# Attention and expert kernel on one core: the scan's filter stored in natural order, the context reversed instead, two heads' filter tiles loaded directly, a paired router, a fifth bank for blocks, and new orders on all engines

## The chip, the cores and the metric

The kernel runs on one core of a Trainium2 chip. The engines are TensorE (PE), VectorE (DVE), ScalarE (ACT), GpSimd (POOL) and SyncE (SP), which issues most DMAs. The metric is the device time of one execution in microseconds.

## What is computed

The reference takes x and a context (8 sequences of 128 channels by 256 steps), normalises x, and combines them in 16 heads of 8 channels: for every pair of channels of a head the product of two context rows is convolved causally with the head's filter, the filter's tap D is added, and the result is multiplied with the query and summed. The result is added to x, normalised again, and goes through a mixture of 8 experts with the best two chosen per row.

```python
kv = einsum('bhil,bhjl->bijhl', k, v)              # k = v = context, by head
y = irfft(rfft(kv, 2L) * rfft(ssm_kernel, 2L))[..., :L]
out = einsum('bijhl,bhil->bjhl', y + kv * D, q)    # q = layernorm(x)
x = x + tanh(g_xattn) * out
z = layernorm(x)
gates = top-2 of softmax(z @ router_w + router_b), normalised
combined = sum over e of gates[e] * gelu(z @ expert_w[e] + expert_b[e])
x = x + tanh(g_ffn) * (combined @ out_w + out_b)
```

## The kernel before, in words

The order of every engine is written out by hand, and the engines meet in semaphores. The program has these stages.

*Start.* Filter taps and D are loaded, VectorE reverses the taps and adds D to the first one, and SP writes them, with 128 zeros behind, to a scratch in DRAM (`kpad_dram`). Five DMAs (`TOEP`) read it back with overlapping rows, which gives the Toeplitz tile `toep` of each head. Context and x come in four loads each (`context_in`, `x_in`), two of each on ScalarE's queue and two on SP's. TensorE transposes the context as it comes (`context(i)`), ScalarE evacuates it to `ctxT`. VectorE takes the statistics of the first four sequences of x, GpSimd the power -1/2 of their variances (`first_inverse_std`), VectorE writes the scaled queries in reversed order (`backwards`), and TensorE transposes them (`queries(i)`). `WARM_UP` says how many transposes without a use TensorE does between these.

*Convolutions.* There are 32 items n: two groups of four sequences (g = n // 16) by 16 heads. `products` multiplies pairs of context channels (on GpSimd, for the items in `BY_VECTOR` on VectorE) into one of six slots, `convolve(n)` is two fp32 products with `toep` into one of four banks (`ring`), and `query_products(n)` on VectorE (four instructions) multiplies with the queries into `zq` and frees the bank (`read_out`).

*Sums.* `sum_channels(b)` adds the slots of `zq` by transposes that accumulate, for one sequence. `fold` adds one half of the slots to the other beforehand, so that fewer transposes are left: one fold in the first group (8 slots become 7), four in the second, two by VectorE and two by GpSimd (`FOLDED_BY_DVE`, `FOLDED_BY_POOL`). `residual(b)` on VectorE adds x from memory and frees the bank of the sum. ScalarE takes statistics, normalises, TensorE transposes z, and high and low parts of z are taken (`z_high`, `z_low`).

*Experts.* A block (b, k) is one sequence by two experts, six matmuls of 512 columns in `experts(n, b, k)`. There are 32, the first 16 for the sequences 0 to 3. ScalarE does the gelu in the bank, VectorE multiplies with the gates and adds (`accumulate`), which frees the bank. The experts' weights are made relative to their last row (`relative`), then split into a high part (ScalarE, `split_weights`) and a low part (`weights_low`). The router has six matmuls (`route_logits`), its logits are transposed back (`route_rows`), and VectorE picks the two best and makes the gates (`choose_values`, `choose_experts`, `weigh`). At last the mixture is transposed, split and projected (`mix_transposed`, `mix_low`, `project`, `finish`).

The sums of the second group stand on TensorE behind the first four blocks, and wait for all folds:

```python
for n in range(4, 7):
    sum_channels(n)        # behind experts(3)
experts(4, *BLOCKS[4])
sum_channels(7)
```

## Time and profile before

| | us |
|---|---|
| median of 3 runs (lowest, highest) | 116.19 (115.92, 118.51) |
| the profiled execution | 115.83 |
| its span, first to last instruction | 114.0 |
| TensorE busy in it | 103.2 |
| VectorE busy | 90.2 |
| GpSimd busy | 63.0 |
| ScalarE busy | 57.2 |

The span is what the views of the trace cover; the 1.8 us between it and the execution's own time lie around it. All times of a row are counted from the span's start. TensorE's busy time counts matmuls that overlap one another, so the distance between the starts of two rows says more about its pace than the length of one. An engine's idle time costs something only where TensorE, or whoever it waits for, is late because of it.

### The profile page before, as it was taken

Reading aid. Unit: us, or ns where it says so; the run is one execution under the profiler, and the core shown is the slowest. Engines: PE = TensorE matmul, PEld = TensorE weight load, DVE = VectorE, ACT = ScalarE, POOL = GpSimd, SP = SyncE. Lnnn points to the kernel's source line nnn. Section 1 sums busy time; section 2 is a strip of 40 time slices with the busy share of each in tenths; the row PEclk is TensorE's granted clock in tenths of the full one; section 3 lists DMA queues with packets and bytes.
Section 4 is the critical chain, followed back from the end, with each engine's and each line's share of the span. In section 5 each row is a group of like instructions: output and inputs, shape, how many; then the busy total and the mean of one; then the engine's idle time right before and its main releaser. Section 6 shows DMA issues by size and latency. Waiting matters only on the chain.

```text
span 114.0 us, 1919 instructions
## 1 busy us (share of the span) xinstructions
PE 103.2 (90%) x574; PEld 86.3 (76%) x574; DVE 90.2 (79%) x293; ACT 57.2 (50%) x145; POOL 63.0 (55%) x83
## 2 busy tenths in 40 slices
PE   4956999989999999996679999999999999999960
PEld 4945888868999887754568888886788888888940
DVE  0283899999999998999889969777588876866940
ACT  4074377064258718641469997465645424353300
POOL 3015799999999999999999899600000000000000
PEclk9999999999999999999999999999999999999997
DMA  2867999159872410030030000000000101111031
GB/s 79 294 165 196 297 370 324 50 180 244 227 231 87 155 35 3 0 92 0 0 95 6 0 0 0 0 0 0 0 6 0 46 11 35 46 49 46 0 98 46
DMA packets 10956, 10.02 MB, mean 88 GB/s; under 512 B 1306, under 2 KB 10946, under 8 KB 10946
## 3 DMA queue, kind: packets, MB, share of 16 engines
q1 hardware_dynamic: 9570, 8.85, 26.6%
q10 hardware_dynamic: 1376, 1.05, 2.9%
q8 instruction: 5, 0.08, 0.3%
q14 instruction: 5, 0.04, 0.1%
HBM read 8.82 MB, written 1.07 MB: 87 GB/s over the span
## 4 chain that ended last, share of the span: by engine, by line
PE 61%; POOL 17%; DVE 13%; ACT 4%; issue 3%; POOLq 0%; DVEq 0%
PE ring L835 11%; PE ring L837 11%; PE ring L836 11%; POOL kv_t L374 10%; PE ring L756 6%; DVE zq_t L397 4%; PE ring L757 3%; PE ring L706 3%; DVE ow_lo_t L1040 2%; POOL w_lo_t L389 2%; ACT q_t L560 2%; PE red L779 2%; POOL rstd L403 2%; PE zbank L877 2%; PE red L712 2%
## 5 line engine op out<-in xcount | busy, mean ns | idle before, releaser
L1116 DVE SCALAR_TENSOR_TENSOR mix_t<-ring,ctxT_t,mix_t 128x256 f32<-128x256 f32 x55 | 26.6, 484 | 7.8 <-ACT ring L603 6.1
L603 ACT ACTIVATE ring<-ring 128x512 f32<-128x512 f32 (+1 forms) x33 | 18.7, 568 | 20.7 <-PE ring L837 20.7
L374 POOL TENSOR_TENSOR kv_t<-ctxT_t 128x320 f32<-128x320 f32 x27 | 23.7, 908 | 8.2 <-ACT ctxT_t L515 6.5
L835 PE MATMUL ring<-w_hi_t,zT_hi_t 128*128 128x512 f32 (+1 forms) x66 | 26.1, 396 | 0.0
L837 PE MATMUL ring<-w_hi_t,zT_lo_t 128*128 128x512 f32 (+1 forms) x66 | 25.4, 385 | 0.0
L836 PE MATMUL ring<-w_lo_t,zT_hi_t 128*128 128x512 f32 (+1 forms) x66 | 25.4, 384 | 0.0
L756 PE MATMUL ring<-kv_t,toep_t 128*128 128x288 f32 x64 | 20.9, 409 | 0.2 <-DVE zq_t L1021 0.2
L757 PEld LDWEIGHTS ring<-kv_t,toep_t 128*128 128x128 f32 x64 | 12.2, 190 | 3.3
L837 PEld LDWEIGHTS ring<-w_hi_t,zT_lo_t 128*128 128x128 f32 x66 | 12.4, 188 | 2.5
L835 PEld LDWEIGHTS ring<-w_hi_t,zT_hi_t 128*128 128x128 f32 x66 | 12.5, 189 | 2.3
L836 PEld LDWEIGHTS ring<-w_lo_t,zT_hi_t 128*128 128x128 f32 x66 | 12.5, 189 | 2.1
L779 PE MATMUL red<-ident,zq_t 128*128 128x128 f32 x88 | 11.3, 280 | 2.7 <-POOL zq_t L397 1.5
L1016 DVE TENSOR_TENSOR zq_t<-ring,qT_t 128x256 f32<-128x256 f32 x32 | 13.3, 415 | 0.1
L779 PEld LDWEIGHTS red<-ident,zq_t 128*128 128x128 f32 x88 | 10.5, 194 | 3.7 <-issue 2.7
L757 PE MATMUL ring<-kv_t,toep_t 128*128 128x144 f32 x64 | 13.1, 286 | 0.0
L1018 DVE TENSOR_TENSOR zq_t<-ring,qT_t 128x192 f32<-128x192 f32 x32 | 11.1, 347 | 0.0
L756 PEld LDWEIGHTS ring<-kv_t,toep_t 128*128 128x128 f32 x64 | 9.9, 191 | 0.4 <-issue 0.4
L389 POOL TENSOR_TENSOR w_lo_t<-ctx_t,w_hi_t 128x512 fp32r<-128x512 f32 x7 | 9.4, 1355 | 0.0
L549 ACT ACTIVATE w_hi_t<-ctx_t 128x512 fp32r<-128x512 f32 x8 | 5.0, 621 | 3.9 <-POOL ctx_t L383 3.9
L706 PE MATMUL ring<-ident 128*128 128x128 f32 x25 | 5.4, 372 | 1.6 <-POOL ident L453 1.6
L397 POOL TENSOR_TENSOR zq_t<-zq_t 128x1024 f32<-128x1024 f32 x2 | 6.7, 3371 | 0.0
L397 DVE TENSOR_TENSOR zq_t<-zq_t 128x1024 f32<-128x1024 f32 x3 | 5.9, 2006 | 0.0
(124 smaller groups left out, 170.8 us busy)
## 6 DMA issues: line engine op xcount, KB each, us to landing
ctx_t<-in_L_ffn_expert_w SPq DMA_DIRECT2D x8, 256.0 KB, 4.3
toep_t<-kpad_dram SPq DMA_DIRECT2D x3, 512.0 KB, 6.6
x_t<-in_x SPq DMA_DIRECT2D x8, 128.0 KB
out<-x_t SPq DMA_DIRECT2D x8, 128.0 KB
wlast_t<-in_L_ffn_expert_w SPq DMA_DIRECT2D x1, 768.0 KB, 7.1
ctx_t<-in_ctx ACTq DMA_DIRECT2D x2, 256.0 KB, 3.0
zq_t<-in_x ACTq DMA_DIRECT2D x2, 256.0 KB, 3.7
ctx_t<-in_ctx SPq DMA_DIRECT2D x2, 256.0 KB, 4.2
```

Source lines behind the costliest of these rows:

```text
L374: eng.tensor_tensor(dst, head.unsqueeze(1).to_broadcast([P, HB + 1, HD * CB]), windows(ctxT_t, g, h, HB + 1), ALU.mult).then_inc(done, 1)
L389: eng.tensor_tensor(w_lo[:, :, e, :], raw[:, e % RAW], w_hi[:, :, e, :].bitcast(F32), ALU.subtract).then_inc(done, 1)
L397: eng.tensor_tensor(terms[:, i], terms[:, i], terms[:, HB + i], ALU.add).then_inc(done, 1)
L603: act.activation(y, y, ACT.Gelu_apprx_tanh).then_inc(gelu_ready, 1)
L756: pe.matmul(y, within, src, start=True, stop=False)
L757: pe.matmul(y[:, :, BG:CB], past, src[:, :, 0:BG], start=False, stop=True).then_inc(convolved, 1)
L779: last = pe.matmul(red[b % 2][:, P * c:P * (c + 1)], zq[:, g, i, :, BG * c + b % BG], ident[:, :], is_transpose=True, start=(i == 0), stop ...
L835: pe.matmul(y, hi, whi, start=(c == 0), stop=False)
L836: pe.matmul(y, hi, wlo, start=False, stop=False)
L837: last = pe.matmul(y, lo, whi, start=False, stop=(c == C - 1))
L1016: dve.tensor_tensor(terms(HB * P, [[P * CB, HB]], H, HD), pairs, windows(qT_t, g, h, HB).rearrange("p d (i a) -> p d i a", i=HD), ALU.mult)
L1116: dve.scalar_tensor_tensor(out=acc, in0=ring[n % RING][:, L * e:L * (e + 1)], scalar=gate, in1=acc, op0=ALU.mult, op1=ALU.add).then_inc(mi ...
```

## The change

The filter is stored in natural order, without VectorE's reversal: the taps are loaded behind 127 zeros, GpSimd adds D, and the halves of the Toeplitz tile change places. What must now be reversed is the context: ScalarE writes each load reversed in time (`turn(i)`), and TensorE transposes that copy. Queries and residuals are no longer reversed. x is first on ScalarE's queue, and the first two context loads go to SP's. The item order within a group begins with head 1 (`FIRST`), and the tiles of heads 1 and 2 (`DIRECT`) don't go through the scratch: one DMA behind the scratch write reads them from the taps in DRAM, GpSimd masks what lies outside, and VectorE adds D (`add_direct`). The first group is no longer folded. The router's high and low parts stand side by side (`rw_pair`), so that four matmuls do what six did; the two halves of the result are added in `route_rows` by products with a doubled identity (`twice`). Block 4 writes to `obank` instead of a ring bank, and the later blocks move up by one bank. VectorE takes over the relative step of experts 1 and 3 and the low part of expert 1 and gives back the low part of expert 5. The orders on all engines are new; TensorE does five blocks before the first two sums of the second group, and VectorE has the low part of the projection behind block 5.

The core of the diff:

```diff
-TOEP = ((0, 1), (1, 3), (4, 4), (8, 4), (12, 4))
-BY_VECTOR = (0, 5, 15, 22, 27)
-
-RELATIVE_BY_DVE, LOW_BY_DVE = (), (5,)
-FOLDED_BY_DVE = ((2,), (2, 3))
+FIRST, DIRECT = 1, 2
+TOEP = ((3, 2), (5, 3), (8, 4), (12, 4), (0, 1))
+BY_VECTOR = (2, 3, 9, 14, 23)
+
+RELATIVE_BY_DVE, LOW_BY_DVE = (1, 3), (1,)
+FOLDED_BY_DVE = ((), (2, 3))
 FOLDED_BY_POOL = ((), (0, 1))
-WARM_UP = (12, 1, 6, 1, 5, 5)
+FOLDS = ((4, 0), (5, 1), (6, 2), (7, 3), (2, 0), (3, 1), (1, 0))
+WARM_UP = (14, 1, 26, 1, 1, 5)
...
+        def item(n):
+
+            return n // H, (n + FIRST) % H
+
+        def block_bank(n):
+
+            return obank if n == RING else ring[(n - (n > RING)) % RING]
...
             sp.wait_ge(scratch_written, 16)
             for i, (h, n) in enumerate(TOEP):
-                src = bass.AP(scratch.tensor, h * (P + L), [[1, P], [P + L, n], [1, L]])
+                src = bass.AP(scratch.tensor, h * (P + L - 1), [[1, P], [P + L - 1, n], [1, L]])
                 sp.dma_start(toep[:, h:h + n, :], src).then_inc(toeplitz_in[i], 16)
-                if i >= len(TOEP) - 3 and i < len(TOEP) - 1:
-                    load(sp, xn, x, x_in, i - len(TOEP) + 5)
...
+            for i in range(2):
+                load(sp, cv, ctx_in, context_in, i)
+            sp.wait_ge(taps_ready, 1)
             sp.wait_ge(constants_ready, 1)
             sp.dma_start(scratch, kpad[:, :]).then_inc(scratch_written, 16)
+            src = bass.AP(ssm_kernel.tensor, FIRST * L - (P - 1), [[1, P], [L, DIRECT], [1, L]])
+            sp.dma_start(toep[:, FIRST:FIRST + DIRECT, :], src).then_inc(direct_in, 16)
             for i in range(2, LOADS):
                 load(sp, cv, ctx_in, context_in, i)
+            for i in range(2, LOADS):
+                load(sp, xn, x, x_in, i)
...
+                pool.wait_ge(direct_in, 16)
+                within = toep[:, FIRST:FIRST + DIRECT, 0:P]
+                pool.affine_select(out=within, in_=within, compare_op=ALU.is_ge, fill=0.0, base=1 - P,
+                                   pattern=[[0, DIRECT], [1, P]], channel_multiplier=1).then_inc(direct_masked, 1)
                 pool.wait_ge(first_queries_ready, BG)
...
-            for i in range(2):
-                load(act, cv, ctx_in, context_in, i)
-            for i in range(2):
-                load(act, xn, x, x_in, i)
+            load(act, xn, x, x_in, 0)
+            load(act, xn, x, x_in, 1)
+            act.dma_start(direct_d, everywhere(ssm_d, FIRST, DIRECT)).then_inc(direct_d_in, 16)
...
+            def turn(i):
+
+                act.wait_ge(context_in[i], 16)
+                start = CB * HD * P + B * L + BL * i * L
+                act.activation(backwards(zq_t, G * CB * HD * P, start),
+                               cv[:, BL * i:BL * (i + 1), :].rearrange("p b (c n) -> p b c n", c=C),
+                               ACT.Copy).then_inc(context_turned, 1)
...
+            def block_bank_free(n):
+
+                if n < RING:
+                    pe.wait_ge(read_out, 2 * H - RING + n + 1)
+                elif n == RING:
+                    pe.wait_ge(z_low_ready, BG - 1)
+                else:
+                    pe.wait_ge(mixed_in, 2 * (n - RING + (n > 2 * RING)))
...
+                both = [rw_pair[:, 2 * E * c:2 * E * (c + 1)] for c in range(C)]
+                pe.matmul(red[0][0:2 * E, :], both[0], zT_hi[:, own, 0, :], start=True, stop=False)
                 for c in range(C):
-                    for n, (w, z) in enumerate(((rw_hi, zT_hi), (rw_hi, zT_lo), (rw_lo, zT_hi))):
-                        last = pe.matmul(red[0][0:E, :], w[:, E * c:E * (c + 1)], z[:, own, c, :],
-                                         start=(c == 0 and n == 0), stop=(c == C - 1 and n == 2))
-                last.then_inc(logits_ready, 1)
+                    pe.matmul(red[0][0:E, :], both[c][:, 0:E], zT_lo[:, own, c, :], start=False, stop=False)
+                pe.matmul(red[0][0:2 * E, :], both[1], zT_hi[:, own, 1, :], start=False,
+                          stop=True).then_inc(logits_ready, 1)
...
-                    last = pe.transpose(red[1][:, E * b:E * (b + 1)], lgT_sb[:, P * b:P * (b + 1)], ident[0:E, 0:E])
+                    last = pe.matmul(red[1][:, E * b:E * (b + 1)], lgT_sb[:, P * b:P * (b + 1)], twice[:, :],
+                                     start=True, stop=True)
...
-            for i in range(LOADS):
+            for i in range(2):
                 context(i)
                 warm_up(WARM_UP[i + 1], ring[RING - 1])
             queries(0)
             queries(1)
-            for n in range(0, 16):
+            context(2)
+            context(3)
...
+            def add_direct():
+
+                dve.wait_ge(direct_masked, 1)
+                dve.wait_ge(added_d_ready, 1)
+                within = toep[:, FIRST:FIRST + DIRECT, 0:P]
+                dve.tensor_tensor(within, within, added_d, ALU.add).then_inc(direct_ready, 1)
```

Two places of the order matter for what follows. The first is TensorE's start. Before, with `red` the banks of the context's transposes, `ring` that of the warm-ups, `zbank` and `obank` those of the queries:

```order
L706 MATMUL ring<-ident 128x128 x12
L712 MATMUL red<-ident,ctx_t 128x128 x4
L706 MATMUL ring<-ident 128x128
L712 MATMUL red<-ident,ctx_t 128x128 x4
L706 MATMUL ring<-ident 128x128 x6
L712 MATMUL red<-ident,ctx_t 128x128 x4
L706 MATMUL ring<-ident 128x128
L712 MATMUL red<-ident,ctx_t 128x128 x4
L706 MATMUL ring<-ident 128x128 x5
L712 MATMUL zbank<-ident,q_t 128x128 x2
```

And now, where `zq_t` holds the turned context:

```order
L762 MATMUL ring<-ident 128x128 x14
L768 MATMUL red<-ident,zq_t 128x128 x4
L762 MATMUL ring<-ident 128x128
L768 MATMUL red<-ident,zq_t 128x128 x4
L762 MATMUL ring<-ident 128x128 x26
L768 MATMUL zbank<-ident,q_t 128x128 x2
L768 MATMUL obank<-ident,q_t 128x128 x2
L768 MATMUL zbank<-ident,q_t 128x128 x2
L768 MATMUL obank<-ident,q_t 128x128 x2
L768 MATMUL red<-ident,zq_t 128x128 x8
L820 MATMUL ring<-kv_t,toep_t 128x288
```

The second half of the context has moved behind the queries, to just before the first convolution, and 26 warm-ups stand where there were six and one and five.

The second place is VectorE behind the last query product of the second group. Before, with the folds on top, the low part of the projection (`ow_lo_t`), and then the choice of experts:

```order
L397 TENSOR_TENSOR zq_t<-zq_t 128x1024 x2
L1040 TENSOR_TENSOR ow_lo_t<-ow_t,ow_hi_t 128x512
L1060 MAX zbank<-red 128x8 x4
...
L1029 TENSOR_TENSOR x_t<-red,x_t 128x256
L1113 TENSOR_SCALAR mix_t<-ring,ctxT_t 128x256
L1116 SCALAR_TENSOR_TENSOR mix_t<-ring,ctxT_t,mix_t 128x256
L1029 TENSOR_TENSOR x_t<-red,x_t 128x256
```

And now:

```order
L428 TENSOR_TENSOR zq_t<-zq_t 128x1024 x2
L1136 MAX zbank<-red 128x8 x4
...
L1189 TENSOR_SCALAR mix_t<-ring,ctxT_t 128x256
L1192 SCALAR_TENSOR_TENSOR mix_t<-ring,ctxT_t,mix_t 128x256
L1189 TENSOR_SCALAR mix_t<-ring,ctxT_t 128x256
L1192 SCALAR_TENSOR_TENSOR mix_t<-ring,ctxT_t,mix_t 128x256
L1105 TENSOR_TENSOR x_t<-red,x_t 128x256 x2
```

The low part of the projection has left this place for one behind block 5, and two blocks are mixed in ahead of the first two residuals. On TensorE the sums of the second group, which were three in one piece (24 transposes) behind block 3 and one behind block 4, now are two behind block 4 and two behind block 5.

## Rows read from the trace of the kernel before

**Rows 1.** Head of the page: busy time, share of the span, instructions of each engine.

```profile
PE 103.2 (90%) x574; PEld 86.3 (76%) x574; DVE 90.2 (79%) x293; ACT 57.2 (50%) x145; POOL 63.0 (55%) x83
```

**Rows 2.** Busy time by stretch: us, engines, granted clock, DMA share, GB/s.

```profile
4.30:7.40 3.10, 3.05 (x16) 2.81 (x14) 1.90 (x7) 0.98 (x3) 0.00 (x0) 1.00 0.54 130
12.40:28.90 16.50, 16.09 (x92) 13.60 (x91) 16.09 (x69) 8.40 (x26) 16.14 (x22) 1.00 0.80 236
28.90:45.50 16.60, 16.53 (x115) 14.65 (x113) 15.92 (x67) 9.46 (x29) 16.36 (x24) 1.00 0.41 125
53.00:59.10 6.10, 3.37 (x26) 2.89 (x25) 5.43 (x24) 2.29 (x8) 6.03 (x7) 1.00 0.15 44
61.40:77.40 16.00, 16.00 (x76) 13.19 (x76) 13.34 (x31) 12.09 (x28) 11.31 (x15) 1.00 0.00 0
```

**Rows 3.** Timeline of the start: start us, duration us, engine, line, operation.

```profile
1.64 2.82 PE L706 MATMUL ring<-ident 128*128 128x128 f32 x12 [1.64 <-POOL ident L453]
5.40 0.43 DVE L966 BATCH_NORM_STATS2 zq_t<-zq_t 128x6 f32<-128x256 f32 x1 [1.26 <-DMA zq_t<-in_x]
6.18 0.64 PE L706 MATMUL ring<-ident 128*128 128x128 f32 x2
6.97 0.38 PE L706 MATMUL ring<-ident 128*128 128x128 f32 x2
9.24 1.02 POOL L403 TENSOR_TENSOR rstd<-vareps,neghalf 128x4 f32<-128x4 f32 x1
12.49 0.65 PE L756 MATMUL ring<-kv_t,toep_t 128*128 128x288 f32 x2
```

**Rows 4.** Timeline of 47 to 65 us: VectorE, GpSimd and TensorE.

```profile
47.53 4.71 DVE L397 TENSOR_TENSOR zq_t<-zq_t 128x1024 f32<-128x1024 f32 x2
47.76 6.71 POOL L397 TENSOR_TENSOR zq_t<-zq_t 128x1024 f32<-128x1024 f32 x2
52.17 2.85 DVE L1040 TENSOR_TENSOR ow_lo_t<-ow_t,ow_hi_t 128x512 fp32r<-128x512 f32 x1
54.62 1.13 PE L779 MATMUL red<-ident,zq_t 128*128 128x128 f32 x8 [1.46 <-POOL zq_t L397]
54.94 0.39 DVE L1060 MAX8 zbank<-red 128x8 f32<-128x8 f32 x4
57.68 0.41 DVE L1029 TENSOR_TENSOR x_t<-red,x_t 128x256 f32<-128x256 f32 x1
62.84 0.39 PE L835 MATMUL ring<-w_hi_t,zT_hi_t 128*128 128x512 f32 x1
64.21 0.39 PE L835 MATMUL ring<-w_hi_t,zT_hi_t 128*128 128x512 f32 x1
```

**Rows 5.** DMA issues with KB and median us to landing; one evacuation of ScalarE.

```profile
ctx_t<-in_ctx ACTq DMA_DIRECT2D x2, 256.0 KB, 3.0
zq_t<-in_x ACTq DMA_DIRECT2D x2, 256.0 KB, 3.7
gains<-in_g_xattn ACTq DMA_DIRECT2D x1, 0.5 KB, 3.9
6.42 0.60 ACT L513 ACTIVATE ctxT_t<-red 128x512 f32<-128x512 f32 x1 [4.42 <-PE red L712]
```

**Rows 6.** Timeline of 28 to 40 us; last row: a form of the groups.

```profile
28.89 5.13 PE L779 MATMUL red<-ident,zq_t 128*128 128x128 f32 x42
30.30 0.79 DVE L1051 CAST rw_hi<-rw_t 128x16 fp32r<-128x16 f32 x1 [0.23 <-POOL rw_t L435]
36.87 0.65 PE L756 MATMUL ring<-kv_t,toep_t 128*128 128x288 f32 x2
38.60 0.41 DVE L1016 TENSOR_TENSOR zq_t<-ring,qT_t 128x256 f32<-128x256 f32 x1
39.40 0.41 DVE L1016 TENSOR_TENSOR zq_t<-ring,qT_t 128x256 f32<-128x256 f32 x1
L389 DVE TENSOR_TENSOR w_lo_t<-ctx_t,w_hi_t 128x512 fp32r<-128x512 f32 x1 | 0.8, 760 | 0.0
```

More of the change, by code:

```diff
@@ L467, in _ @@
+            products(pool, 15, pool_products_ready)
+            products(pool, 16, pool_products_ready)
+            relative(pool, 0, weights_relative)
+            for n in range(17, 20):
                 products(pool, n, pool_products_ready)
+            weights_low(pool, 0, weights_low_ready)
+            products(pool, 20, pool_products_ready)
+            relative(pool, 2, weights_relative)
             ones()
-            router_relative_rows()
-            products(pool, 23, pool_products_ready)
@@ L482, in _ @@
-            relative(pool, 2, weights_relative)
-            relative(pool, 3, weights_relative)
-            weights_low(pool, 2, weights_low_ready)
+            products(pool, 21, pool_products_ready)
+            products(pool, 22, pool_products_ready)
+            products(pool, 24, pool_products_ready)
+            weights_low(pool, 2, weights_low_ready)
+            for n in range(25, 29):
+                products(pool, n, pool_products_ready)
+            router_relative_rows()
+            scales(2)
@@ L647, in _ @@
             activate(3)
+            activate(4)
+            split_weights(6)
+            projection_high()
             statistics(B + 4)
-            split_weights(4)
-            statistics(B + 5)
-            statistics(B + 6)
-            activate(4)
-            split_weights(5)
-            statistics(B + 7)
             activate(5)
-            split_weights(6)
+            for n in range(5, 8):
+                statistics(B + n)
             activate(6)
@@ L775, in sum_channels @@
                     pe.wait_ge(pool_folded, sum(len(i) for i in FOLDED_BY_POOL[:g + 1]))
[L776 removed]
+                gone = [FOLDS[i][0] for i in FOLDED_BY_DVE[g] + FOLDED_BY_POOL[g]]
+                slots = [i for i in range(HD) if i not in gone]
                 for c in range(C):
```

364 lines of the change are left out of this document (194 added, 170 removed).

## The prediction

> **What bounds the kernel now.** The first view to read is the head of the page [rows 1]: TensorE is busy 103.2 us (90% of the span), VectorE 90.2. That alone says little, so the second is the busy time by stretch [rows 2]. It cuts the run at the places where the character changes. From 12.4 us to 45.5 TensorE has work almost without a break (16.09 of 16.50, 16.53 of 16.60). From 53.0 to 59.1 it has 3.37 of 6.10, and after 61.4 it is full again (16.00 of 16.00). VectorE is as full up to 59 us (16.09, 15.92, 5.43), and only after that it has slack (13.34 of 16.00). So there are three places where time can come from: the start, up to the first convolution; TensorE's hole of 53 to 59 us; and work taken off TensorE. An edit on another engine pays only through one of these.
>
> The third view is the timeline of the start [rows 3]. VectorE begins the statistics of x at 5.40, when x lands. GpSimd takes a product first and comes to its power of the variance only at 9.24 (1.02 us); the scale, four query rows and their transposes follow, and the first convolution runs at 12.49. Call that moment T.
>
> The fourth is the timeline around the hole [rows 4]. VectorE ends its last query product at 47.5 and starts two folds (4.71 us), while GpSimd does two (6.71 us). GpSimd's second ends at 54.5, and TensorE, which has run out of blocks, starts the channel sums of the second group at 54.62. The third sum waits again, because its bank is read by the residual of 57.68, which stands on VectorE behind the low part of the projection (52.17, 2.85 us) and the gates (from 54.94). The seventh expert block (n = 6) starts at 62.84.
>
> **The start.** x is first on its queue: issued at 0.74 instead of 1.78. The context took 3.0 us from that place, x 3.7 us from the later one [rows 5], so x is there at about 3.7. Four rows of statistics (0.43 and a short aggregation each, some 0.52) and the variance end at 6.0 [rows 3]. GpSimd has no product ahead of its power now, but it has the masking of D, which waits for a small load: issued at about 1.8 with the 3.9 us of the gains [rows 5] that is 5.7, and with 0.3 to 0.6 us for the mask 6.2. So the power runs 6.3 to 7.3. The scale also needs the tanh on ScalarE, and that stands behind the turned context: two loads issued at 1.6 and 2.1 on SP land like x did (5.3 and 5.9); two turns of 128x512. The trace has no turn; the nearest row is ScalarE's copy of 128x512 out of a bank, 0.60 us [rows 5], and the bounds are half of it, if reading elsewhere is cheaper, and twice, if the reversed order halves the rate. I take 0.55. Transposes to 7.0; half the evacuation is that copy and one of half its size, to 7.85; tanh and scale are tiny, 8.35; the query rows are ready at 9.1 and 9.75. TensorE does 26 warm-up transposes after the context's: at 0.11 us (two in 0.38, of which the last lasts 0.27 [rows 3]) that is 7.1 to 9.96. Then 16 transposes (queries 0 and 1, context 2 and 3), 1.75 us: T = 11.7, 0.8 earlier. The first GpSimd product is there by 10.7. The direct Toeplitz load is issued at 4.5, lands with the 3.0 to 3.7 us of the other loads by 8.2, and its mask (to 8.8) and the adding of D on VectorE (half of the 0.76 of a piece twice as large [rows 6]; 1.1 if GpSimd holds it up) end by 11.3: hidden, with 0.4 to spare.
>
> **The convolutions.** The fold of the first group goes, so each of its four sums has 16 matmuls instead of 14: 8 x 0.122 (42 in 5.13) = +1.0 us on TensorE [rows 6]. Before, convolution 21 and the four sums lay between T and 36.87, 24.4 us, with 0.4 idle; now 24.4 + 1.0 - 0.4 = 25.0, the end of convolution 21 being T + 25.0 = 36.7. The two relative steps and the low weights that VectorE takes over lie before that, where it has 10.1 us for 8.0 (alone) to 11.5 us (all held up by GpSimd) of work: I take 0, the end is +1.4. From there VectorE leads: 11 query products at 0.79 to 0.80 (38.60 to 39.40), the router's split 1.4 (two pieces, 0.79 the first), four low parts at some 0.33 (estimated from the 0.41 of a residual, which overlaps the next [rows 4]), together 11.4 [rows 6]. The last product ends at S = T + 36.4 = 48.1; it was 47.5. So half a microsecond is lost here in spite of the earlier start.
>
> **The hole.** Both engines fold from S on, as before; that GpSimd has relative steps and low weights ahead of it changes nothing as long as they end before S (its last product needs convolution 25, about 40; after it stand one low and two relative pieces, some 4 us). GpSimd ends S + 6.9 = 55.0. Until then TensorE has five blocks instead of four, since the fifth has a bank of its own, at 1.37 each (62.84 to 64.21), four logit matmuls at 0.23 instead of six, and rows of 0.6: from 45.5, when the first low part is there, to 53.9. Two sums (16 x 0.115) to 56.8. Gates: VectorE is free at S + 4.6, the low projection no longer stands there, and 54.94 to 57.68 is 2.7 us, so 55.4; the first block is mixed in at 56.4, in time for block 5 at 56.8 to 58.2. The residual of the first sum is done at 57.7, so sums 6 and 7 follow without a wait: block 6 starts at 60.1 against 62.84. That is -2.75 us at this point, front, slots and hole together.
>
> A rule bears on the term of 6.9. The trace first: the low projection took 2.85 us beside GpSimd's folds, where low weights of the same size took 0.76 [rows 4, 6]. The Trainium skill (SBUF — State Buffer, "SBUF: two separate sides") says that a VectorE instruction with two SBUF inputs and a GpSimd instruction exclude each other for the whole instruction. By that rule the trace agrees, and removing the projection takes nothing off GpSimd; by a sharing in proportion GpSimd would end half a microsecond earlier, and the sum would be 112.3.
>
> **The second half.** Four logit matmuls instead of six again: -0.46. The four transposes to rows become fp32 products; a convolution of that type has two records per product, so eight of some 0.06 to 0.09 for four: +0.25. Net -0.2. Projections and transposes of the mixture are interleaved otherwise, with the same number of instructions; TensorE had no idle time there, so at best 0, at worst 0.5 where a block now waits for its mix.
>
> **Sum.** -2.75 - 0.2 = -3.0 us. The profiled execution took 115.83 us (span 114.0), and the median of the three timings is 116.19, lowest 115.92, so it is a typical run: 115.83 - 3.0 = 112.8 us, 2.6% less. About 2% is what a measurement of this kernel can tell from no change, that is 2.3 us.
>
> **Rivals.**
> *The clock comes up late.* The granted clock reads 1.00 from 4.3 to 7.4 [rows 2], but in it two transposes at 6.18 take 0.64 together and two at 6.97 take 0.38: they follow each other at 0.213 us until about 6.8 and at 0.11 afterwards, the 1.2 and 2.4 GHz levels; TensorE had worked without a break since 1.64, 5.1 us [rows 3]. Now it stands still from about 4.9 to 5.85, as the turned context is late. If it takes 5.1 us again from there, the rise comes at 10.95: 15 warm-ups at 0.213, 11 at 0.11 end at 12.15, and with 16 transposes T is 13.9. All behind moves with T: 112.8 + 2.2 = 115.0. For it: the new pause; against it: 14 warm-ups have come before. The Trainium skill (TensorE: Matmul & The Clock Gate, "What's actually happening") holds that low is the default and activity lifts it, at a moment that varies between runs; it speaks for this rival.
> *The first group of blocks after the sums is held up.* The low projection, now behind block 5 on VectorE, can take up to 2.85 us again while GpSimd works, so block 10, due at 65.6, waits for the mix of block 6, and ScalarE has four statistics, two splits and three normalisations there. Price 1.2: 114.0.
> *Slower than before.* The clock stays low until the convolutions: context transposes to 7.75, 26 warm-ups at 0.213 to 13.3, 16 transposes to 16.7, so T is 4.2 later than it was, and the end 112.8 + 5.0 = 117.8, more when convolutions too run at half rate. It decides from T = 14.7 on (no gain left). Against it: before, the clock was up long before this.
> *The fifth bank brings nothing alone.* It only fills a wait that ends with GpSimd's folds; if VectorE and GpSimd meet less in the folds, these end 1.3 earlier and TensorE's 53.9 decides: 111.7.
>
> **Chances.** Forecast 0.50 (own range 111.8 to 113.9), late clock 0.22, held-up blocks 0.16, slower 0.06, better 0.06. Faster by over 2% means below 113.5: 0.43 of the forecast's, the better case and some of the held-up one: 0.53. Slower by over 2% needs the slow start in full, with half-rate convolutions, or another loss of its kind: 0.06. The rest, 0.41, is within 2%. The range: below 111.2 everything would have to go right at once; the late clock with an idle or two reaches 115.5.
>
> **What would show it.** Right: first convolution near 11.7; a gap of TensorE ahead of the first context transposes, with the pitch already 0.11 in the 26 warm-ups; last query product near 48.1; channel sums from 55.0 with a wait of about 1 us for GpSimd's fold; block 6 near 60.1; no wait for residuals in the middle. Wrong: a pitch of 0.21 after 8 us; a wait of TensorE for VectorE in the first blocks after the sums; VectorE's relative steps near 1.5 us a pair, with convolution 21 past 37.5; a hole of more than 2 us before 55.

## The result, and the profile after

The changed kernel takes 118.23 us (median of four, 117.90 to 118.70), the kernel before on the same chip 116.12. The ratio is 1.019, 95% interval 1.016 to 1.022: 1.9% slower, where 112.8 us and 2.6% faster were forecast. The profiled execution took 117.90 us with a span of 116.1. Executions more than 1.5% above the fastest of their kernel are left out of all ratios here; in e1 those are three of four, and no ratio is given for it.

The head of the page shows that TensorE is still the full engine (compare [rows 1]), with 3.2 us more of work and a span 2.1 us longer:

```profile
PE 106.4 (92%) x602; PEld 90.4 (78%) x602; DVE 90.6 (78%) x295; ACT 60.0 (52%) x149; POOL 62.0 (53%) x83
```

Three moments split the run: T, the first convolution; S, the start of VectorE's folds; and the start of block 6 (n = 6). After the change S is right behind the last query product. Before, two low parts stand between them: the last product ends at 46.95 and the folds start at 47.53, so the 47.5 that the prediction calls the end of the last product is S as meant here, and its sum stands. The stretches between them hardly depend on each other, so a change can be read stretch by stretch.

| | T | S - T | block 6 - S | rest of the span |
|---|---|---|---|---|
| before | 12.49 | 35.04 | 15.31 | 51.2 |
| forecast | 11.7 | 36.4 | 12.0 | 51.0 |
| after | 14.81 | 38.00 | 11.87 | 51.4 |

The start after, from the timeline (start us, duration, engine, line, operation), against [rows 3]:

```profile
1.70 3.25 PE L762 MATMUL ring<-ident 128*128 128x128 f32 x14 [1.70 <-POOL ident L488]
...
5.99 0.63 ACT L569 ACTIVATE zq_t<-ctx_t 128x512 f32<-128x512 f32 x1 [3.92 <-DMA ctx_t<-in_ctx]
...
6.67 1.11 PE L768 MATMUL red<-ident,zq_t 128*128 128x128 f32 x4 [1.72 <-ACT zq_t L569]
...
7.85 0.63 ACT L569 ACTIVATE zq_t<-ctx_t 128x512 f32<-128x512 f32 x1 [1.24 <-DMA ctx_t<-in_ctx]
...
8.53 1.12 PE L768 MATMUL red<-ident,zq_t 128*128 128x128 f32 x4 [0.54 <-ACT zq_t L569]
...
9.44 3.79 PE L762 MATMUL ring<-ident 128*128 128x128 f32 x26
...
10.44 0.20 ACT L672 ACTIVATE tgains<-gains 128x2 f32<-128x2 f32 x1
...
11.03 1.39 DVE L1073 TENSOR_SCALAR q_t<-zq_t,mv,qscale 128x256 f32<-128x256 f32 x4
...
13.07 0.38 PE L768 MATMUL zbank<-ident,q_t 128*128 128x128 f32 x2
...
14.81 0.65 PE L820 MATMUL ring<-kv_t,toep_t 128*128 128x288 f32 x2
```

Read the brackets first: ScalarE waits for the context's DMA, TensorE for ScalarE. TensorE stands still from 4.95 to 6.67. Then read durations: four transposes take 1.11 us, at 0.213 us from one to the next, the 1.2 GHz level; before, two took 0.38 from 6.97 on [rows 3]. The 26 warm-ups take 3.79 us instead of the 2.86 that 0.11 each would make. The pages' lists of DMA issues have the context's landing. Before, the first two loads took 3.0 us on ACT's queue [rows 5], and the two later ones, on SP's, took 4.2. Now all four are on SP's queue, with a median of 5.1; the first two, which matter here, took 4.3 and 5.7 (issued at 1.68 and some 0.5 later, there at 5.99 and 7.85). The first row is from before, the second from after:

```profile
ctx_t<-in_ctx SPq DMA_DIRECT2D x2, 256.0 KB, 4.2
ctx_t<-in_ctx SPq DMA_DIRECT2D x4, 256.0 KB, 5.1
```

Between T and S, VectorE has the pieces taken over from GpSimd. The timeline has them, with some query products left out:

```profile
30.00 1.40 DVE L404 TENSOR_TENSOR ctx_t<-ctx_t,wlast_t 128x256 f32<-128x256 f32 x1
31.33 1.05 DVE L405 TENSOR_TENSOR ctx_t<-ctx_t,wlast_t 127x256 f32<-127x256 f32 x1
...
34.38 0.67 DVE L404 TENSOR_TENSOR ctx_t<-ctx_t,wlast_t 128x256 f32<-128x256 f32 x1
34.97 1.05 DVE L405 TENSOR_TENSOR ctx_t<-ctx_t,wlast_t 127x256 f32<-127x256 f32 x1
35.95 1.33 DVE L411 TENSOR_TENSOR w_lo_t<-ctx_t,w_hi_t 128x512 fp32r<-128x512 f32 x1
```

That is 5.5 us, against 0.76 us for a piece of the last kind before [rows 6]. Two rows show their effect. TensorE ends convolution 21 where the next one starts, at 40.28, and VectorE comes to query product 21 only at 41.36:

```profile
40.28 0.65 PE L820 MATMUL ring<-kv_t,toep_t 128*128 128x288 f32 x2
...
41.36 0.41 DVE L1093 TENSOR_TENSOR zq_t<-ring,qT_t 128x256 f32<-128x256 f32 x1
```

VectorE is 1.1 us behind there, and it is busy without a gap to S. The hole of [rows 4] is gone: one short wait is left, and the low projection, now later, takes 0.75 instead of 2.85.

```profile
52.81 4.53 DVE L428 TENSOR_TENSOR zq_t<-zq_t 128x1024 f32<-128x1024 f32 x2
...
52.86 6.75 POOL L428 TENSOR_TENSOR zq_t<-zq_t 128x1024 f32<-128x1024 f32 x2 [2.21 <-DVE zq_t L1098]
...
59.75 2.01 PE L844 MATMUL red<-ident,zq_t 128*128 128x128 f32 x16 [0.16 <-POOL zq_t L428]
...
64.68 0.47 PE L903 MATMUL ring<-w_hi_t,zT_hi_t 128*128 128x512 f32 x1
...
66.64 0.75 DVE L1116 TENSOR_TENSOR ow_lo_t<-ow_t,ow_hi_t 128x512 fp32r<-128x512 f32 x1
```

And the rows of the router, from its last logit matmul to the next block's first:

```profile
52.51 0.40 PE L870 MATMUL red<-zT_hi_t,rw_pair 128*16 128x512 f32 x1
...
54.22 1.05 PE L878 MATMUL red<-twice,qT_t 16*128 16x8 f32 x8
55.20 0.50 PE L903 MATMUL ring<-w_hi_t,zT_hi_t 128*128 128x512 f32 x1
```

So the gain of the hole came (-3.4 us) and two losses ate it: 2.3 us at the start and 3.0 us in the convolutions. The rest of the span adds 0.2.

### The profile page after: what moved, and what is told of

Its sections match the earlier page's. It is cut to its first block, busy times and chain, and to the rows that moved or that the text cites. A ratio compares the mean times of both kernels' runs of the same rounds, so it can differ in the third digit from the quotient of the medians.

```text
span 116.1 us, 1985 instructions
## 1 busy us (share of the span) xinstructions
PE 106.4 (92%) x602; PEld 90.4 (78%) x602; DVE 90.6 (78%) x295; ACT 60.0 (52%) x149; POOL 62.0 (53%) x83
## 3 DMA queue, kind: packets, MB, share of 16 engines
HBM read 8.82 MB, written 1.07 MB: 85 GB/s over the span
## 4 chain that ended last, share of the span: by engine, by line
PE 51%; DVE 20%; POOL 11%; issue 7%; DMA 5%; ACT 2%; SPq 1%; DVEq 0%; POOLq 0%
PE ring L903 11%; PE ring L905 11%; PE ring L904 11%; DVE zq_t L1093 6%; DMA ctx_t<-in_ctx 5%; DVE zq_t L1095 4%; POOL zq_t L428 4%; PE red L844 3%; PE ring L762 3%; POOL kv_t L396 2%; DVE zq_t L1097 2%; DVE ctx_t L405 2%; PE red L768 2%; DVE zq_t L1098 2%; PE zbank L945 2%
## 5 line engine op out<-in xcount | busy, mean ns | idle before, releaser
L1192 DVE SCALAR_TENSOR_TENSOR mix_t<-ring,ctxT_t,mix_t 128x256 f32<-128x256 f32 x53 | 25.5, 483 | 7.9 <-ACT ring L658 6.5
L658 ACT ACTIVATE ring<-ring 128x512 f32<-128x512 f32 (+1 forms) x32 | 18.1, 568 | 20.3 <-PE ring L905 20.3
L903 PE MATMUL ring<-w_hi_t,zT_hi_t 128*128 128x512 f32 (+1 forms) x64 | 25.6, 400 | 0.3 <-DVE zT_lo_t L1110 0.3
L905 PE MATMUL ring<-w_hi_t,zT_lo_t 128*128 128x512 f32 (+1 forms) x64 | 24.6, 385 | 0.0
L904 PE MATMUL ring<-w_lo_t,zT_hi_t 128*128 128x512 f32 (+1 forms) x64 | 24.6, 384 | 0.0
L820 PE MATMUL ring<-kv_t,toep_t 128*128 128x288 f32 x64 | 21.4, 416 | 1.4 <-DVE zq_t L1098 1.4
L903 PEld LDWEIGHTS ring<-w_hi_t,zT_hi_t 128*128 128x128 f32 x64 | 12.0, 188 | 2.7 <-DVE zq_t L1098 0.5
L844 PEld LDWEIGHTS red<-ident,zq_t 128*128 128x128 f32 x96 | 11.2, 191 | 0.8 <-issue 0.6
L762 PE MATMUL ring<-ident 128*128 128x128 f32 x41 | 7.5, 355 | 1.7 <-POOL ident L488 1.7
L762 PEld LDWEIGHTS ring<-ident 128*128 128x128 f32 x41 | 6.8, 191 | 1.7 <-POOL ident L488 1.7
```

What stands on the lines that cost most here:

```text
L658: act.activation(y, y, ACT.Gelu_apprx_tanh).then_inc(gelu_ready, 1)
L762: pe.transpose(bank[:, 0:P], ident[:, :], ident[:, :])
L820: pe.matmul(y, within, src, start=True, stop=False)
L844: last = pe.matmul(red[b % 2][:, P * c:P * (c + 1)], zq[:, g, i, :, BG * c + b % BG], ident[:, :], is_transpose=True, start=(i == 0), stop ...
L903: pe.matmul(y, hi, whi, start=(c == 0), stop=False)
L904: pe.matmul(y, hi, wlo, start=False, stop=False)
```

## The experiments

### The start: e1, e2, e3

e1 takes warm-ups away where they seem to hold the queries, e2 adds some where TensorE stands still.

```diff
-WARM_UP = (14, 1, 26, 1, 1, 5)
+WARM_UP = (14, 1, 6, 1, 1, 5)      # e1
+WARM_UP = (22, 1, 26, 1, 1, 5)     # e2
```

e3 puts the context back at the head of ACT's queue:

```diff
+            for i in range(2):
+                load(act, cv, ctx_in, context_in, i)
             load(act, xn, x, x_in, 0)
             load(act, xn, x, x_in, 1)
-            for i in range(2):                      # on SP
-                load(sp, cv, ctx_in, context_in, i)
```

> The changed kernel with 6 instead of 26 warm-up transposes behind context(1). Theory A (they only stand in front of the query transposes, which could start at 12.42 us when the queries are written): first convolution at about 14.2 us instead of 14.81, held by 8 query and 8 context transposes of 0.11 us each and by product(0), which ends at 13.55; device time about 117.6 us. Theory B (they are what brings the granted clock up, since TensorE stood still from 4.95 to 6.67 us): TensorE has no work from about 11 to 12.4 us, the 16 transposes take 0.21 to 0.27 us each, the first convolution starts at 16 us or later, device time 119 us or more.

> The changed kernel with 22 instead of 14 warm-up transposes ahead of context(0), so that TensorE works through to 6.67 us. Theory B (the pause of 1.72 us is what keeps the clock down until 11 us): the granted clock rises before 7 us as in the kernel before, context(0) and (1) take 0.66 instead of 1.11 us, the 26 warm-ups 2.8 instead of 3.79 us, the queries start at about 12.0 instead of 13.07 and the first convolution at about 13.9 instead of 14.81; device time about 117.2 us. Rival (the late landing of the context alone, 5.99 and 7.85 us, sets the start): the first convolution stays within 0.3 us of 14.81, device time 118.0 us.

> The changed kernel with its first two context loads back at the head of ACT's queue and x behind them. Theory (the queue order is the whole of the late start): turn(0) starts by 4.0 us and turn(1) by 5, TensorE doesn't stand still for more than 0.5 us before 6 us, the clock rises before 7 us, x's statistics start at 5.4 us, the first convolution starts at 12.5 to 13.0 us, device time 115.8 to 116.3 us. Rival (the direct Toeplitz load, the two turns and the 26 warm-ups are late by themselves): the first convolution at 14 us or later, device time 117.3 us or more.

Measured. e1: three executions took 118.3 to 118.6 us, as the change does, and one took 116.4; the profile is of 118.6, so nothing shows what the fourth did otherwise. In the profile the query transposes take 0.69 us for two, T is 15.17 and the first convolution itself runs at half rate (1.17 us instead of 0.65). It is theory B, with T 0.8 us short of its bound. e2: 116.3 us profiled, ratio to before 1.003 (0.998 to 1.008), so no loss that the measurement can tell is left, with eight useless transposes more. From its timeline:

```profile
1.70 4.10 PE L762 MATMUL ring<-ident 128*128 128x128 f32 x22 [1.70 <-POOL ident L488]
...
6.59 0.66 PE L768 MATMUL red<-ident,zq_t 128*128 128x128 f32 x4 [0.79 <-ACT zq_t L569]
...
7.93 0.66 PE L768 MATMUL red<-ident,zq_t 128*128 128x128 f32 x4 [0.57 <-ACT zq_t L569]
...
8.42 3.00 PE L762 MATMUL ring<-ident 128*128 128x128 f32 x26
...
13.32 0.72 PE L820 MATMUL ring<-kv_t,toep_t 128*128 128x288 f32 x2 [0.16 <-POOL kv_t L396]
```

The four transposes take 0.66 us, as the clock came up at 4.7 us, and T is 13.32, 1.5 us earlier. Not all of that is the clock: the second turn of the context starts at 7.24 here and at 7.85 in the change, because its load landed earlier. e6, e7 and e8 below have the same start as e2, and show both effects:

| start of e2, profiled in | second turn starts | transposes 0.21 us apart again | T |
|---|---|---|---|
| e2 | 7.24 | no | 13.32 |
| e8 | 8.09 | no | 14.17 |
| e6 | 8.01 | from 9.0 | 15.43 |
| e7 | 8.49 | from 9.5 | 15.92 |

```profile
8.09 0.63 ACT L569 ACTIVATE zq_t<-ctx_t 128x512 f32<-128x512 f32 x1 [2.22 <-DMA ctx_t<-in_ctx]
...
14.17 0.72 PE L820 MATMUL ring<-kv_t,toep_t 128*128 128x288 f32 x2 [0.16 <-POOL kv_t L396]
```

(The lines are e8's.) With the clock up in both, e8's turn is 0.85 us later than e2's, and so is T. With the turn at the same place, e6 is 1.3 us later than e8, by the clock. For the change, with its turn at 7.85, that makes T an estimated 13.9 with the clock up: 0.9 of its 14.81 is the clock. And e2's 13.32 is the best of four, in its landing and in its clock. e3: ratio 1.001 (0.998 to 1.005), T 13.71, a smaller gain than expected. TensorE has no pause, though the clock comes up only at about 7.6 us (the expectation had it before 7), and now x lands at 6.36 (5.40 before [rows 3]; 5.64 in e11, which has the same start) and the tanh comes at 9.16, when the last of the three small loads behind x on that queue, of D and the gains, has landed. Context and x can't both be first on one queue, and what goes second pays about two microseconds (x: 6.36 against 3.98 where it was in front).

### The pieces on VectorE: e4, e6

e4 leaves work out of the change, to have its price; e6, on e2, gives two pieces to GpSimd.

```diff
-            relative(dve, 1, dve_weights_relative)   # and 3
+            touch(1, dve_weights_relative)           # e4: 8 columns
```

```diff
-RELATIVE_BY_DVE, LOW_BY_DVE = (1, 3), (1,)
+RELATIVE_BY_DVE, LOW_BY_DVE = (3,), ()               # e6
             relative(pool, 0, weights_relative)
+            relative(pool, 1, weights_relative)
...
+            weights_low(pool, 2, weights_low_ready)  # from ahead of products(25)
             weights_low(pool, 3, weights_low_ready)
             relative(pool, 4, weights_relative)
-            relative(pool, 5, weights_relative)
             fold(pool, 1, 0, pool_folded)
             fold(pool, 1, 1, pool_folded)
+            relative(pool, 5, weights_relative)
```

> Leaves out nearly all of relative(1) and relative(3) on DVE (8 of 512 columns each stand for them), so their experts' weights stay as loaded. Theory (DVE sets the end of the query products, S, and the pieces stand there at their full 4.14 us): S comes 3.7 us earlier (49.1 instead of 52.8). Behind it the GpSimd folds can start only 2.2 us earlier, since GpSimd waited 2.21 us for S: device time 116.0 us. Rival (convolutions and GpSimd's products pace the query products): S earlier by less than 2 us, device time above 117 us.

> The kernel of e2_bridge with relative(1) and the low weights of expert 1 on GpSimd instead of VectorE; for that GpSimd's low weights 2 stand behind its last product and relative(5) behind the folds. Theory (VectorE sets the end S of the query products, and beside GpSimd it pays 1.40 + 1.05 + 1.33 us for pieces that cost GpSimd 0.73 + 0.73 + 1.27): S comes 2.5 to 3.8 us earlier than 51.2; GpSimd's folds start at about 50.0 instead of 51.3 since GpSimd is then the full one, block 6 starts 1.2 us earlier (61.9), 115.1 us. Rival (GpSimd's products pace the convolutions as soon as it gets more): S within 1 us of 51.2 and the time no better than 116.3.

Measured. e4 left out less than it was meant to: with only 8 columns, the first piece still took 1.17 us. It started 0.12 us behind a GpSimd instruction and ended with it:

```profile
30.27 1.26 POOL L411 TENSOR_TENSOR w_lo_t<-ctx_t,w_hi_t 128x512 fp32r<-128x512 f32 x1
30.39 1.17 DVE L1118 TENSOR_TENSOR ctx_t<-ctx_t,wlast_t 128x8 f32<-128x8 f32 x1
```

The other took 0.26 us, and the low weights, no longer beside the same instructions, 0.68 instead of 1.33; together the pieces shrank from 5.5 to 2.1 us. S - T is 35.6 instead of 38.0, so 2.4 of these 3.4 us came back, and VectorE now waits 1.3 us for the sums. The time, 115.8 us, is 0.989 of before (0.978 to 1.000). The expectation was met in the time; its 3.7 us in S were not, as S lies between the theory and the rival. e6: S - T is 36.3 (-1.7), and GpSimd's wait ahead of its folds falls from 2.21 to 0.56 us. Its device time, 116.8 us, is no better than e2's, as in the profiled execution T was 15.43: the clock had fallen again (below). In the stretch the theory holds at two thirds of its smaller figure (1.7 of 2.5 us); the time doesn't show it.

### The clock again: e5, e12

Both start from e2 and take the tanh ahead of the evacuation. e5 also has 12 warm-ups instead of 26 and the later context's transposes behind convolution 2; e12 keeps TensorE at work in both pauses: `WARM_UP = (30, 12, 12, 1, 1, 5)`.

> The kernel of e2_bridge (first convolution at 13.32 us, 116.3 us profiled) with the tanh of the gains ahead of the context's evacuation on ScalarE, 12 instead of 26 warm-ups behind context(1), and context(2), (3) transposed behind convolution 2. Theory (after the clock, T is set by the order in which small work stands in front of the queries): tanh at 8.1 instead of 9.38, query rows ready at 9.9 instead of 11.3, product(0) from 10.4, first convolution at 11.5 to 11.8; all behind it moves, 114.6 us. Rival (the clock isn't up by then, or the masked direct tile is late: its load lands near 9.7): T above 12.8, above 115.8 us.

> The kernel of e2_bridge with TensorE kept at work in both pauses (30 warm-ups ahead of context(0), 12 instead of 1 ahead of context(1), 12 instead of 26 behind it) and the tanh ahead of the evacuation. Theory (every pause lets the clock fall or delays its rise; in e5 and e6 it fell again behind 8 us, after pauses of 0.85 and 0.97 us): every transpose after 7 us runs at 0.11 us, the first convolution at 12.3 to 12.7 us in every run, so the runs lie within 0.3 us of each other, at 115.3 to 115.7 us. Rival (the clock goes by something else than the pauses): runs spread over more than 0.8 us as those of e2, with some of 0.21 us a transpose behind 8 us.

Measured. e5: 117.5 us, the rival. The windows of its profile (us; busy of PE, PEld, DVE, ACT, POOL; granted clock; DMA share; GB/s) show why:

```profile
7.00:8.00 1.00, 0.55 (x5) 0.31 (x3) 0.00 (x0) 0.17 (x1) 0.86 (x1) 1.00 0.78 206
8.00:9.00 1.00, 0.49 (x3) 0.49 (x4) 0.30 (x2) 0.55 (x2) 0.00 (x0) 0.73 0.95 294
9.00:10.00 1.00, 1.00 (x6) 1.00 (x6) 1.00 (x4) 0.33 (x1) 0.28 (x1) 0.50 1.06 368
...
11.00:12.00 1.00, 1.00 (x7) 1.00 (x6) 0.66 (x2) 0.31 (x2) 0.55 (x1) 0.56 0.98 335
```

The clock had come up, and after two pauses of 0.85 and 0.97 us it was granted at half, 1.2 GHz, from 8.5 to past 11 us. Pauses alone don't say when it falls: before, a pause of 1.37 us (7.35 to 8.72) and in e9 one of 1.79 us left the clock up, and in e8 it came up around one of 1.07 us, with the transposes 0.21 us apart until 7.3 and 0.11 apart behind it. Besides, S - T rose to 39.5; TensorE waited 0.85 us ahead of queries(2), for ScalarE. That this comes from the second context being transposed later is likely, but wasn't looked into. e12: in the profiled execution every transpose behind 7 us takes 0.11 us, and the eight executions lie within 0.6 us (116.4 to 117.0), where those of e2 spread over 1.0; the clock part of the theory holds, though not to the 0.3 us it gave. The time doesn't: ratio 1.004 (1.002 to 1.006). T is 13.10, as the masked tile's addition on VectorE takes 1.05 us beside a GpSimd product, and contexts 2 and 3 are transposed at 12.09; and S - T is 38.6. With the clock up T still follows the load that lands late: the second turn starts at 8.13, and 12 warm-ups stand ahead of its transposes until 9.25.

### Router, low projection: e7, e8

e7 has six logit matmuls and the transposes back; e8 puts `projection_low()` back ahead of `choose_values(0)`. Both on e2.

> The kernel of e2_bridge with the router as it was: six logit matmuls, four transposes to rows. By the prediction's term the pair of hi and lo columns is worth 0.46 a group less 0.25 for the rows, so this costs 0.2 us in each of the two groups. By the trace after (rows 0.98 us for four products where the transposes took 0.34) the pair loses in each group 0.64 - 0.46 = 0.18 us: from block 6 to the end 0.2 us less, 116.1 us. In the first group no change is expected, since TensorE waits for GpSimd's fold there (0.16 us).

> The kernel of e2_bridge with the low part of the projection back where it was, behind VectorE's folds and ahead of the gates (and its high part behind the bias on ScalarE). Theory (the exclusive use of the buffer by GpSimd, as before): the piece takes about 2.9 us there instead of 0.75, GpSimd's folds still end at 58.0, the gates come 2.9 us later (58.6), blocks are mixed in 2.9 us later, so block 5 and sums 6, 7 wait: block 6 at 65.0 to 65.5 instead of 63.1, device time 118 us. Rival (the wait was only a matter of banks, which the fifth bank has cured): block 6 within 0.5 us of 63.1.

Measured. e7: its rows stand between 55.51 and 55.85, 0.34 us, against 0.98 with the pair; block 6 to the end takes 51.27 instead of e2's 51.49, so the pair costs some 0.2 us. (The profile is of an execution of 118.55 us, long because of its start, T = 15.92; in time, 1.004 of before against e2's 1.003, it is too small to see.) e8: 119.3 us, ratio 1.027 (1.021 to 1.032); block 6 - S is 14.07 instead of 11.87, and T is 14.17, 0.9 us of its loss against e2.

```profile
56.58 2.88 DVE L1116 TENSOR_TENSOR ow_lo_t<-ow_t,ow_hi_t 128x512 fp32r<-128x512 f32 x1
59.38 0.39 DVE L1136 MAX8 zbank<-red 128x8 f32<-128x8 f32 x4
...
63.02 0.50 PE L903 MATMUL ring<-w_hi_t,zT_hi_t 128*128 128x512 f32 x1 [1.02 <-DVE mix_t L1192]
```

The piece takes 2.88 us here, the gates come by so much later, and block 5 waits for the mix of block 0. Moving this one line is worth 2.2 us of the 3.4. (Its high part moved with it, on ScalarE.)

### The hole's part alone: e9, e10

e9 is the kernel before with `block_bank` and the order behind it, and nothing else of the change; e10 folds three on VectorE, one on GpSimd.

```diff
+            weights_low(pool, 3, weights_low_ready)
             fold(pool, 1, 0, pool_folded)
             fold(pool, 1, 1, pool_folded)      # e10: on VectorE
-            weights_low(pool, 3, weights_low_ready)
...
-            experts(3, *BLOCKS[3])
-            for n in range(4, 7):
-                sum_channels(n)
-            experts(4, *BLOCKS[4])
-            sum_channels(7)
+            for n in range(2, 5):
+                experts(n, *BLOCKS[n])
+            sum_channels(4)
+            sum_channels(5)
+            experts(5, *BLOCKS[5])
+            sum_channels(6)
+            sum_channels(7)
```

> The kernel before with only the second part of the change: the fifth block's bank, the order behind it (two sums, block 5, two sums, gates without the low projection ahead of them), the low weights of expert 3 ahead of GpSimd's folds. Start, filter, queries, first group's fold, shares of VectorE and six logit matmuls as before. Theory (the parts add up by stretches, and the hole's part is worth what it was in the change): first convolution 12.49, S 47.5 as before; GpSimd's folds start 1.3 us later (49.0) and end at 55.8, then two sums, a block, two sums as after (5.1 us): block 6 at 60.9 instead of 62.84, device time 113.9 us, 1.7% below before. Rival (the gain of the hole needs the rest of the change): block 6 later than 62.3, time within 0.5 us of 115.9.

> The kernel of e9_hole_only with three of the four folds on VectorE and one on GpSimd. Theory A (an instruction of one engine excludes the other's while it runs, so the folds' time adds up: 1.2 us for one of VectorE's, (6.7 - 2.4)/2 = 2.15 for one of GpSimd's): the folds and the low weights ahead of them end about 0.9 us earlier (54.9 instead of 55.8), block 6 at about 60.0, device time 113.0 us. Theory B (both engines simply run slower beside each other, 2.3 us each for VectorE's): VectorE's three folds end at about 54.5, the gates at 57.2, 2 us later than in e9, block 5's partners come late: block 6 at 61 or later, 114 us or more.

Measured. e9: T 12.28, block 6 at 60.66 (60.9 expected), 114.8 us profiled where 113.9 was expected. Of ten executions three took 114.8 to 115.0 and the others 116.1 and more, so the ratio is 0.997 (0.992 to 1.001). Block 6 - S is 13.30, 2.0 us less than before and not 3.4, and the rest of the span is 1.0 us longer. One wait is new, for VectorE's low weights of expert 5:

```profile
55.68 2.04 PE L790 MATMUL red<-ident,zq_t 128*128 128x128 f32 x16 [0.54 <-POOL zq_t L401]
...
60.66 0.48 PE L846 MATMUL ring<-w_hi_t,zT_hi_t 128*128 128x512 f32 x1
...
64.28 0.47 PE L846 MATMUL ring<-w_hi_t,zT_hi_t 128*128 128x512 f32 x1 [0.63 <-DVE w_lo_t L393]
```

e10: 115.5 us, with block 6 at 61.67, 1.0 later than in e9. Both theories held a half. The folds end 1.0 us earlier (54.5 instead of 55.5), as A has it, but all on VectorE, which therefore makes the gates 3.6 us later, and block 5 waits for the mix:

```profile
58.46 0.50 PE L845 MATMUL ring<-w_hi_t,zT_hi_t 128*128 128x512 f32 x1 [1.29 <-DVE mix_t L1127]
```

The work that two engines do at each other's cost can be shifted between them, but it should end on the one that nobody waits for.

### Together: e11, e13, e14, e15

e11 is the change with e3, e6 and e7. e13 moves expert 5's low weights to GpSimd in e9, e14 fills the pause ahead of context(2) with 12 more warm-ups, e15 reorders GpSimd behind that:

```diff
             weights_low(pool, 4, weights_low_ready)
+            weights_low(pool, 5, weights_low_ready)  # e13
-            add_bias(0)
-            add_bias(1)
-            weights_low(pool, 6, weights_low_ready)
             relative(pool, 7, weights_relative)
             scales(3)
+            weights_low(pool, 6, weights_low_ready)  # e15
             weights_low(pool, 7, weights_low_ready)
-            for n in range(2, 8):
+            for n in range(0, 8):
```

> The changed kernel with its context first on ACT's queue (e3), the pieces on GpSimd (e6) and six logit matmuls (e7). If the terms add: first convolution 13.7, S 36.3 behind it = 50.0, block 6 at 61.9, the rest 51.6: span 113.5, device time 115.3 us against 116.4 of e3. Rival (GpSimd, with no wait left, now sets S or the blocks behind the folds): 116 us or more.

> The kernel of e9_hole_only with the low weights of expert 5 on GpSimd behind those of expert 4 (ready at about 62.3) instead of on VectorE, where block 8 waited 0.63 us for them (62.54, 1.59 us). Expected: no wait at block 8, 0.6 us less than e9: 114.2 us where e9 had 114.8, and 115.6 where it had 116.3, if e9's two levels of time remain. If the levels stem from something that this step had to do with, they go.

> The kernel of e13_low5_pool with 18 instead of 6 warm-ups behind context(1), so that TensorE works through its pause of 1.79 us (6.74 to 8.53 in e9) until context(2) lands. Theory (e9's two levels, 114.9 and 116.3 us, are executions whose clock stays up or falls in that pause, as it did in e5 behind 8 us): all executions at the lower level, within 0.5 us of each other, 114.2 us. Rival (the levels come from elsewhere, the landing of loads for example): both levels still there, 1.4 us apart.

> The kernel of e13_low5_pool, whose wait of 0.63 us at block 8 went and came back as 0.86 us ahead of the transposes of z(4) (the second group's scales were pushed back on GpSimd), with relative(7) and the scales ahead of the low weights 6 and 7 and all bias additions behind them. Expected: the scales 1.9 us earlier (64.6 instead of 66.5), no wait ahead of z(4), 0.9 us less than e13: 114.4 us. Rival (the normalisation waits for ScalarE's statistics, not for GpSimd): no gain, 115.3 us.

Measured. e11: 115.8 us, ratio 0.995 (0.993 to 0.998), with T 13.29 and S - T 37.2. The terms don't add in full (S - T was to be 36.3): TensorE now waits 0.8 us in that stretch for a product of GpSimd. e13: 115.3 us, 114.2 or 115.6 being expected. The wait at block 8 went and came back, larger, three blocks later:

```profile
68.76 0.44 PE L803 MATMUL zbank<-ident,q_t 128*128 128x128 f32 x2 [0.86 <-ACT q_t L567]
```

e14: 115.3 us, all six within 0.2. e13 has the pause and has no second level either (one execution took 116.1, but its span is 113.5 like the others'), so e14 can't tell what e9's second level was; that stays open. e15: the scales come at 64.45 instead of 66.50, the wait is gone, block 6 to the end takes 51.3 instead of 52.7, and the time is 113.84 us (113.36 to 114.76), 0.979 of before (0.974 to 0.983), faster than both kernels. It is 0.6 better than expected: block 11 starts 1.7 us behind block 10 instead of 3.1, a gain larger than the wait of 0.86. Of the change, e15 keeps only the fifth bank and the order behind it; the start, the filter and the queries are those of before.

```profile
55.91 2.03 PE L789 MATMUL red<-ident,zq_t 128*128 128x128 f32 x16 [0.57 <-POOL zq_t L401]
...
60.89 0.48 PE L845 MATMUL ring<-w_hi_t,zT_hi_t 128*128 128x512 f32 x1
...
64.45 0.20 POOL L415 TENSOR_SCALAR vareps<-sumsq 128x4 f32<-128x4 f32 x1 [0.62 <-ACT junk L537]
```

## Why the prediction was wrong, step by step

The sum missed by 5.1 us (117.9 against 112.8): 3.1 at the start, 1.6 in the convolutions, -0.1 in the hole (block 6 - S: 12.0 forecast, 11.9 measured), 0.4 in the rest; what is missing to 5.1 is rounding.

*The start, "T = 11.7" (14.81).* The steps on x were right: the power ran from 6.71 (forecast 6.3). The step that failed is "two loads issued at 1.6 and 2.1 on SP land like x did (5.3 and 5.9)": they landed at 5.99 and 7.85. The tanh, behind the turns and the evacuation, came at 10.44 instead of 7.85, and the query rows with it. The forecast took x's 3.7 us from ACT's queue, where the page of before had 4.2 us for the same load on SP's. Why they took 4.3 and 5.7 isn't shown: both queues now had large loads on their way at once, but no run takes that apart from the place on SP's queue, and the same start lets the second turn begin anywhere from 7.24 to 8.49 (the table under e2). The direct Toeplitz load was late too (9.6 instead of 8.2), but didn't hold T. Then "at 0.11 us (...) that is 7.1 to 9.96" put the warm-ups at the high clock. The rival with the late clock had the mechanism, from the same pause, and a T of 13.9; it was given 0.22. By the table under e2 the clock made 0.9 us of the 3.1 and the landing about 2. The rivals were priced as alternatives to an early context, though the two go together: a later context is a longer pause. A case with both had no price.

The Trainium skill (TensorE: Matmul & The Clock Gate, "What's actually happening") says that the low state is the default, that work lifts it, and that the moment varies from run to run. The runs agree: with the same program up to there, the 26 warm-ups took 3.79 us after the change and 4.81 in e4, and with e2's start the clock came up at 4.7 us in e2, 5.4 in e6, 5.9 in e7 and behind 7.3 in e8.

*The convolutions, "I take 0" (1.6).* VectorE's work up to the end of convolution 21 was bounded at 8.0 to 11.5 us in 10.1 us, and taken to fit. The pieces came near the upper bound: 1.05 to 1.40 us for most, 5.5 in all. The 0.76 of [rows 6] was of a piece that hardly met a GpSimd instruction; here GpSimd was busy without a gap from 29.85 to 38.4 us, so meeting one is the rule. The end of convolution 21 was forecast at T + 25.0 and came at T + 25.5 (40.28). The other 1.1 us is the step "From there VectorE leads: 11 query products": at that moment it still had product 20 and a residual to do. e4 shows 2.4 us for pieces shorter by 3.4. The forecast had named the sign ("relative steps near 1.5 us a pair"), though the pairs took 2.45 and 1.72.

*The hole (right).* Sums with 0.16 us of wait, block 6 11.87 behind S, the low projection 0.75 us in its new place. e8 confirms that this line alone is 2.2 us. In e9 the part without the rest is worth 2.0 us up to block 6 and gives 1.0 of it back behind; e15 gets that back. By the Trainium skill (SBUF — State Buffer, "SBUF: two separate sides") a two-input VectorE instruction and a GpSimd one take turns as wholes; e10 agrees, as the folds' work ended 1.0 us earlier by moving one to the engine that does it in less time, 0.9 being expected from that rule, and so does e4's piece of 8 columns, which lasted as long as the GpSimd instruction beside it.

*The second half, "Net -0.2" (+0.2).* The matmuls saved 0.46 as said. The term mis-sized is "eight of some 0.06 to 0.09 for four: +0.25": the rows take 0.98 us where the transposes took 0.34, +0.64. e7 gives 0.2 us back.

*The slower rival* had the right sign and nearly the right time (117.8), by luck, as it took another route, "the clock stays low until the convolutions", T = 16.7. That is what e1 shows, with T at 15.17; in the change the clock came up at about 11.3 us. The blocks behind the sums had no wait, so the second rival didn't happen here; in e9 and e13 waits of its kind did.

## What to carry to other kernels

Cut the run at a few moments that everything passes and compare stretch by stretch: ten of the profiles here have 11.85 to 11.90 us for the third stretch, with first convolutions from 12.9 to 15.9. A load that comes later costs its own delay, one for one where everything waits for it (e2, e8), and can cost the clock of TensorE on top (e6: 1.3 us): look at what TensorE does in every pause of the start. Keeping it at work made the executions alike (e12), though not faster than e2's. Take one profiled start for a sample: the same program had T from 13.3 to 15.9 us. And price a piece moved to VectorE at what it costs beside a busy GpSimd, and move only the piece whose new place nobody waits for.

## What the runs showed of the hardware

TensorE's clock fell, after it had come up, around pauses of less than 1 us each with little work between them (e5: 0.85 and 0.97 us, then 0.50 granted from about 8.5 us past 11; e6 alike), and stayed up through longer ones elsewhere (1.37 us before, 1.79 in e9). At the very start, though, the granted clock reads 1.00 in the windows while transposes follow each other at 0.213 us (after, 6.67 to about 11 us): there the durations tell the level, not the column. Four products with 16 rows and 8 columns took 0.98 us, 0.25 each (two records each, 0.11 us apart), where a transpose of 8 rows took 0.085. A VectorE instruction of 8 columns took 1.17 us beside a GpSimd instruction of 1.26 and 0.26 at another place (e4), so next to a busy GpSimd a small piece isn't a cheap one.
